# Routing 29 of 32 token tiles before the block boundary, with constant matmuls on a waiting TensorE

## The chip, the cores and the metric

The kernel runs on one core of a Trainium2 chip. The metric is the device time of one execution in microseconds, and lower is better. Three runs of the kernel before took 1498.8, 1500.05 and 1500.13 us; the median is 1500.05. The engines are TensorE (PE in the rows, with PEld for its weight loads), VectorE (DVE), ScalarE (ACT), GpSimd (POOL) and SyncE (SP), which here issues DMAs.

## The reference

The input x has 8 x 512 rows of 1024 numbers. Two stages are added to it one after the other:

```python
x = x + tanh(g_xattn) * long_conv(ctx, ctx, layernorm(x), ssm_kernel, D)   # head size 8
x = x + tanh(g_ffn) * moe(layernorm(x), G, gate_w, up_w, down_w, lora_A, lora_B)
```

The long convolution stands where attention would: the products of keys and values within a head are convolved with a kernel of 1024 steps and contracted with the queries. In the mixture of experts each of the 4096 rows (tokens) gets scores by a softmax over 8 experts; its two best experts (the first of equals) each compute down(silu(gate x) * (up x)) with 128 hidden units and a low-rank term of rank 16, weighted by the score:

```python
scores = softmax(x @ G); value, indices = top_k(scores, 2)
w = sum_k value_k * one_hot(indices_k)
out = einsum('bsef,bse,ehf->bsh', silu(gate) * up, w, down_w) + lora term
```

## The kernel before

The kernel is written directly for the engines: each has its own list of instructions, and semaphores order them. There are two blocks. At the end of a block all engines meet (line L199 in the rows), so that no engine starts the second block before all have issued what they have in the first.

**First block, `attend`.** It runs over 32 tiles (NT) of 128 rows: two plain passes, a loop, and two plain ones for tiles 30 and 31. Per tile TensorE computes the convolution as fp32r products of 288 columns (`conv`, `shared`), VectorE multiplies with the queries and sums (`multiply`, `total`, `residual`), ScalarE and GpSimd split numbers in high and low parts. One and two tiles later follow the second norm (`root2`, `invert2`, `normalize2`), its transposes (`transpose_n2`), the high and low parts (`high_n2`, `low_n2`), and the product with G (`project`, `take_small`, `turn`, `take_lr`), which leaves the tile's 8 logits per token in `logits`. After tile 31's convolution this tail runs once more with nothing beside it. SyncE stores the new x and the normed rows n2 of tile 31 and waits until they have landed.

**Second block, `route_tokens`, then `experts_on_slots`.** The routing computes, for all 32 tiles at once and for 256 elements per partition, the softmax and the two one-hot choices (VectorE, about 20 operations that each wait for the one before), and counts on TensorE (CNT) how many tokens go to each expert ahead of each token. From the counts it makes each choice's slot tile and row in it. It then builds `is_slot` and `is_row` on VectorE (L947, L952), multiplies is_slot by the token's number on GpSimd (`slot_number`, L1018), and 64 matmuls of 72 columns (IDX, L1054) turn them into the list of tokens per slot. From IDX come `token` (L966), which GpSimd's indirect DMAs need to gather rows (L826), and the tables of experts and waits (L971 to L978), which end with `tables_done`. Only then do the slots start: 71 slots of 128 rows, each transposed (L1228), multiplied with its expert's weights (L1241 to L1260) and scattered (L1112). The gathered row holds the token's 8 weights as well, so that the gathers wait until they have been stored (`weight_out`, L987).

SyncE in the second block first copies rows to a spare place (L981), loads two experts' weights (L813), waits for each, stores the weights of the routing (L987), and then issues the packs: 16 DMAs of 64 KB (`pack`, L799) that bring the low-rank matrices, split in high and low parts by the first block, together in DRAM, from where `load_b` takes them (L804).

Of the kernel before, what the change touches and what calls it, by code (L numbers as in the profile page):

```python
# [21 lines left out]
F32 = mybir.dt.float32  # L22
# [43 lines left out]
BACK = SLOTS // NB  # L66

# [6 lines left out]
class Constants:  # L74


    def __init__(self, nc, ctx, g_xattn, g_ffn, ident, order, utri, ones, iota, grid, number):
# [7 lines left out]
        self.first = [(self.ident, ident), (self.g_xattn, g_xattn)]  # L85
        self.later = [(self.g_ffn, g_ffn), (self.order, order), (self.utri, utri), (self.ones, ones), (self.iota, iota),
# [3 lines left out]
def attend(nc, logits, constants, x_d, c_d, k_d, dskip_d, ag_d, w_d, khi_d, klo_d, kshi_d, kslo_d, out_d, normed_d, whi_d, wlo_d):  # L90
# [3 lines left out]
    with ctx:  # L94
# [8 lines left out]
        kvhi = [sb(f"kvhi{h}", [P, NC, YC], F32R) for h in range(HT)]  # L103
        kvlo = [sb(f"kvlo{h}", [P, NC, YC], F32R) for h in range(HT)]
# [41 lines left out]
        shared_y = view(OP[:], [[HALF, 2], [1, YC]])  # L146

# [43 lines left out]
        q_done = sem("q_done")  # L191

# [6 lines left out]
        with nc.Block() as block:  # L199

            @block.sync
            def _(eng):
# [64 lines left out]
                body(NT - 1, 1, last=True)  # L267
                eng.wait_ge(res_done, NT)
# [6 lines left out]
                eng.wait_ge(w_out, 32 * NT)  # L275
                eng.wait_ge(later_in, 16 * len(constants.later))

            @block.gpsimd
            def _(eng):
# [50 lines left out]

                head(0, 0, 0, 16)

# [12 lines left out]
                body(NT - 1, 1, NT // 2 - 1, last=True)  # L345

            @block.scalar
            def _(eng):
# [110 lines left out]
                eng.wait_ge(const_in, 48)  # L459
                nc.scalar.activation(gt[:], gate[:], ACT.Tanh).then_inc(gate_ready, 1)  # L460
                nc.scalar.copy(ag_parts[:, :, 0, :], ag[:]).then_inc(ag_split, 1)
# [5 lines left out]
                def body(i, p, k, first=False, last=False):  # L467
# [11 lines left out]
                    take_common(2 * i + 1, 1)  # L479
                    if not last:  # L480
                        head(2 * i + 2, 1 - p, 0)
# [12 lines left out]
                body(NT - 1, 1, NT // 2 - 1, last=True)  # L494
                take_small(NT - 2)
                root2(NT - 1, 1)
                normalize2(NT - 1, 1)
                high_n2(NT - 1)
                take_small(NT - 1)

            @block.vector
            def _(eng):
# [86 lines left out]
                def body(i, p, k, first=False, last=False):  # L589
# [19 lines left out]
                    total(i, p, 1, 0)  # L609
                    if not first:  # L610
                        low_n2(i - 1)
# [11 lines left out]
                body(NT - 2, 0, NT // 2 - 1)  # L623
# [6 lines left out]
                take_lr(NT - 1)  # L630

            @block.tensor
            def _(eng):
# [90 lines left out]
                eng.wait_ge(const_in, 48)  # L724
# [31 lines left out]
                body(NT - 1, 1, last=True)  # L756
                transpose_o(NT - 1, 1)
                project(NT - 2)
                turn(NT - 2)
                transpose_n2(NT - 1, 1)  # L760
                project(NT - 1)
                turn(NT - 1)


class Chosen:


    def __init__(self, nc, ctx):
        sb = lambda n, s, dt=F32: ctx.enter_context(nc.sbuf_tensor(n, s, dt))
        U32 = mybir.dt.uint32  # L770
        self.token, self.dest = sb("token", [P, SG], U32), sb("dest", [P, SG], U32)
        self.spare_out, self.tables_done = ctx.enter_context(nc.semaphore("spare_out")), ctx.enter_context(nc.semaphore("tables_done"))
        self.need = sb("need", [P, NB, SG], mybir.dt.int32)
        self.opened = sb("opened", [1, NB, E])
        self.scattered = [ctx.enter_context(nc.semaphore(f"scattered{b}")) for b in range(NB)]
        self.own = sb("own", [P, SG, E])
        self.table = sb("table", [P, 2, SG], mybir.dt.int32)
        self.ends = sb("ends", [P, E], mybir.dt.int32)


class Weights:


    def __init__(self, nc, ctx):
        sb = lambda n, s, dt=F32: ctx.enter_context(nc.sbuf_tensor(n, s, dt))
        self.hi = sb("wt_hi", [P, 2, WC], F32R)
        self.lo = sb("wt_lo", [P, 2, WC], F32R)
        self.lb = ctx.enter_context(nc.sbuf_tensor("lora_b", [P, 2, L], F32R))
        self.landed = ctx.enter_context(nc.semaphore("weights_landed"))
        self.lb_zero = ctx.enter_context(nc.semaphore("lb_zero"))  # L790
        self.lb_landed = ctx.enter_context(nc.semaphore("lb_landed"))
        self.packed = ctx.enter_context(nc.semaphore("packed"))

    def pack(self, eng, w_d, b_d, e):

        part = bass.AP(tensor=w_d.tensor, offset=w_d.offset + NT // E * e * P * WT + WQ,
                       ap=[[WT, P], [P * WT, NT // E], [1, BQ]])
        to = bass.AP(tensor=b_d.tensor, offset=b_d.offset + e * R * L, ap=[[NT // E * BQ, P], [BQ, NT // E], [1, BQ]])
        eng.dma_start(to, part).then_inc(self.packed, 16)  # L799

    def load_b(self, eng, bhi_d, blo_d, e):

        for n, d in enumerate((bhi_d, bhi_d, blo_d)):
            eng.dma_start(self.lb[n * ST:n * ST + R, e % 2, :].bitcast(F32), d[e]).then_inc(self.lb_landed, 16)  # L804

    def load(self, eng, whi_d, wlo_d, e, singly=False):
# [597 lines left out]
```

## Time and profile before

| | us |
|---|---|
| median of three runs | 1500.05 |
| the profiled execution | 1499.49 |
| its span, first to last instruction | 1497.7 |
| TensorE busy | 1398.2 (93%) |
| VectorE busy | 1152.2 (77%) |
| ScalarE busy | 774.7 (52%) |
| GpSimd busy | 1117.3 (75%) |
| mean granted TensorE clock | 0.970 of 2.4 GHz |

The profile shows one execution. Its 40 slices of 37.4 us each give the busy share of each engine in tenths:

```profile
PE   3999999999999999999999999933899999999994
DVE  3999999999999999999999999958354454445452
POOL 6998999899899989998999899515355555555552
PEclk9999999999999999999999999955999999999997
```

A 9 is 90% or more. TensorE is full everywhere but at the start, at the end and in two slices between the attention and the slots, where the granted clock (PEclk, in tenths of full) is also low. The time is thus the sum of two stages that TensorE bounds and of the stretch between them.

### The profile page before, as it was taken

The page shows a single profiled execution, that of the slowest core. Times are in us where ns is not written, and L with a number is a line of the kernel's source. Part 1 is how long each engine was busy: PE and PEld are TensorE (multiplying, and loading weights), DVE is VectorE, ACT ScalarE, POOL GpSimd, SP SyncE. Part 2 cuts the span into 40 slices and gives each one's busy share as a digit, 9 for nine tenths or more (in the row PEclk, how much of TensorE's full clock was granted, in tenths as well). Part 3 has the DMA queues.
Part 4 walks back from the last instruction along what each step waited for, and adds up shares of the span by engine and source line. Part 5 has one row for each costly group of instructions (what it writes and reads, how often), then busy time and mean ns, then how long its engine had stood idle before and what let it go on. Part 6 is the DMA issues. An engine that isn't in the chain of part 4 may idle for free. (4 is left out here: it accounts for less than half of the span.)

```text
span 1497.7 us, 33735 instructions
## 1 busy us (share of the span) xinstructions
PE 1398.2 (93%) x10290; PEld 1347.3 (90%) x10291; DVE 1152.2 (77%) x1922; ACT 774.7 (52%) x1359; POOL 1117.3 (75%) x985
## 2 busy tenths in 40 slices
PE   3999999999999999999999999933899999999994
PEld 3999999999999999999999999923899999999994
DVE  3999999999999999999999999958354454445452
ACT  5656665666566656665666566410333443343341
POOL 6998999899899989998999899515355555555552
PEclk9999999999999999999999999955999999999997
DMA  6766675777676767676767676436589999999984
GB/s 202 206 217 224 213 229 207 231 207 234 204 228 210 235 201 226 211 228 210 227 210 233 203 226 212 161 130 169 120 199 251 267 232 238 250 271 217 234 179 72
DMA packets 114342, 315.44 MB, mean 211 GB/s; under 512 B 25152, under 2 KB 25664, under 8 KB 114304
## 3 DMA queue, kind: packets, MB, share of 16 engines
q1 hardware_dynamic: 93728, 239.96, 50.9%
q0 software_dynamic: 20576, 75.04, 22.4%
q8 instruction: 16, 0.26, 0.1%
q14 instruction: 22, 0.18, 0.0%
HBM read 215.66 MB, written 100.86 MB: 211 GB/s over the span
## 5 line engine op out<-in xcount | busy, mean ns | idle before, releaser
L536 DVE TENSOR_REDUCE oT<-z 128x128 f32<-128x1280 f32 x256 | 380.5, 1486 | 8.9
L637 PE MATMUL Y<-kvhi,t_hi 128*128 128x288 f32 x1280 | 382.5, 299 | 0.0
L638 PE MATMUL Y<-kvlo,t_hi 128*128 128x288 f32 x1280 | 377.7, 295 | 0.0
L639 PE MATMUL Y<-kvhi,t_lo 128*128 128x288 f32 x1280 | 377.1, 295 | 0.0
L309 POOL TENSOR_TENSOR kvlo<-kv,kvhi 128x1152 fp32r<-128x1152 f32 x128 | 340.7, 2686 | 0.0
L292 POOL TENSOR_TENSOR kv<-cT 128x768 f32<-128x768 f32 x128 | 239.1, 1868 | 9.1 <-DMA cT<-in_c 9.1
L637 PEld LDWEIGHTS Y<-kvhi,t_hi 128*128 128x128 f32 x1280 | 240.5, 188 | 0.6
L638 PEld LDWEIGHTS Y<-kvlo,t_hi 128*128 128x128 f32 x1280 | 240.8, 188 | 0.0
L639 PEld LDWEIGHTS Y<-kvhi,t_lo 128*128 128x128 f32 x1280 | 240.8, 188 | 0.0
L519 DVE TENSOR_TENSOR z<-Y,qT 128x512 f32<-128x512 f32 x256 | 176.8, 691 | 28.2 <-PE Y L639 16.2
L1241 PE MATMUL GU<-wt_hi,xu_hi 128*128 x568 | 170.5, 300 | 0.0
L1243 PE MATMUL GU<-wt_lo,xu_hi 128*128 x568 | 164.4, 290 | 0.0
L1242 PE MATMUL GU<-wt_hi,xu_lo 128*128 x568 | 163.5, 288 | 0.0
L637 PE MATMUL Y<-kvhi,u_hi 128*128 128x288 f32 x512 | 155.0, 303 | 0.0
L1109 POOL TENSOR_TENSOR clear<-own 1x1 f32<-1x1 f32 x284 | 44.2, 183 | 144.2 <-issue 115.1
L639 PE MATMUL Y<-kvhi,u_lo 128*128 128x288 f32 x512 | 151.3, 295 | 0.0
L638 PE MATMUL Y<-kvlo,u_hi 128*128 128x288 f32 x512 | 151.1, 295 | 0.0
L303 POOL TENSOR_TENSOR diff<-kv 128x576 f32<-128x576 f32 x64 | 92.1, 1439 | 65.8 <-ACT kv L353 62.9
L364 ACT CAST kvhi<-kv 128x1152 fp32r<-128x1152 f32 x128 | 140.8, 1149 | 0.4 <-POOL kv L295 0.4
L522 DVE TENSOR_TENSOR z<-Y,qT 128x384 f32<-128x384 f32 x256 | 140.4, 549 | 0.0
L1112 POOL DMA_INDIRECT out<-made,dest x71 | 113.0, 1591 | 27.0 <-issue 19.7
L515 DVE TENSOR_TENSOR Y<-Y,common 128x576 f32<-128x576 f32 x128 | 97.9, 765 | 36.1 <-PE Y L639 36.1
(174 smaller groups left out, 3266.4 us busy)
## 6 DMA issues: line engine op xcount, KB each, us to landing
cT<-in_c SPq DMA_DIRECT2D x32, 768.0 KB, 8.0
t_hi<-khi SPq DMA_DIRECT2D x64, 384.0 KB, 3.6
t_lo<-klo SPq DMA_DIRECT2D x64, 384.0 KB, 5.0
u_hi<-kshi SPq DMA_DIRECT2D x64, 320.0 KB, 5.8
u_lo<-kslo SPq DMA_DIRECT2D x64, 320.0 KB, 6.8
x_nat<-in_x SPq DMA_DIRECT2D x32, 512.0 KB, 4.1
out<-x_new SPq DMA_DIRECT2D x32, 512.0 KB, 4.8
normed<-n SPq DMA_DIRECT2D x32, 512.0 KB, 7.4
```

The costliest lines, as they stand in the source:

```text
L292: nc.gpsimd.tensor_tensor(view(o, [[YC, NC // 2], [IB, ND - 1], [1, IB]], IB), view(cc, [[WR, NC // 2], [0, ND - 1], [1, IB]]), view(cc, [ ...
L309: nc.gpsimd.tensor_tensor(kvlo[h][:, c0:c0 + NC // 2, :], kv[:, c0:c0 + NC // 2, :], kvhi[h][:, c0:c0 + NC // 2, :].bitcast(F32), ALU.subt ...
L364: nc.scalar.copy(kvhi[h][:, c0:c0 + NC // 2, :], kv[:, c0:c0 + NC // 2, :]).then_inc(kvhi_done, 1)
L519: nc.vector.tensor_tensor(view(zz, [[ZC, 2], [2 * SK, ND], [2, IB]]), view(y, [[HALF, 2], [IB, ND], [1, IB]]), view(q, [[WR, 2], [0, ND], ...
L522: nc.vector.tensor_tensor(view(zz, [[ZC, 2], [2 * IB, ND - 1], [2, IB]], 1), view(y, [[HALF, 2], [IB, ND - 1], [1, IB]], IB), view(q, [[WR ...
L536: nc.vector.tensor_reduce(oT[p][:, 2 * r:2 * r + 2, h * IB:(h + 1) * IB], view(z[s][:], [[ZC, 2], [2, IB], [2 * IB, ZS], [1, 2]]), AX.XY, ...
L637: nc.tensor.matmul(out, w_hi[:, w], m_hi[:, c, :], start=start, stop=False)
L638: nc.tensor.matmul(out, w_hi[:, w], m_lo[:, c, :], start=False, stop=False)
L639: return nc.tensor.matmul(out, w_lo[:, w], m_hi[:, c, :], start=False, stop=stop)
L1241: nc.tensor.matmul(out, xt_hi[p][:, c, :], wh, start=c == 0, stop=False)
L1242: nc.tensor.matmul(out, xt_lo[p][:, c, :], wh, start=False, stop=False)
L1243: mm = nc.tensor.matmul(out, xt_hi[p][:, c, :], wl, start=False, stop=c == NC - 1)
```

## The change

The change does the following.

- **29 tiles routed in the first block.** TE is 29, TL is 3. Tiles 0 to 28 (early) get their softmax, choices, counts and places within `attend`: `start_early` in VectorE's tile 30, Exp in ScalarE's tile 31, the rest between the steps of tile 31's tail, and their counts in TensorE's tail into a free half of Y[0]. GpSimd multiplies the early weights (`product`) and makes the early row matrices of two of four pieces (`number_rows`, 29 operations of 128 elements) before the blocks meet.
- **3 tiles late.** The second block handles tiles 29 to 31 in operations of 24 elements, and one matmul brings in the early sums. The prefix sum over the experts takes two operations instead of eight.
- **The number moves.** The row matrix now holds the token's number (is_equal, then mult, in one operation), in the buffers of kvhi and kvlo; `slot_number` on GpSimd falls away. One of the four pieces is made on ScalarE as Square and Relu (32 operations), the others on GpSimd.
- **SyncE.** In the first block it now waits for the early weights, stores them, and only then stores x and n2 of tile 31; after their landing it issues all 16 packs. In the second block it waits for the packs, then loads, with the late weights' store in between.
- **Constant products.** `keep_busy` issues matmuls of 256 columns whose output nothing reads: 40 before transpose_o of tile 31, 30 before transpose_n2, 3 before the last turn; in the second block 25 before the late counts, 40 before IDX, 55 after it.
- **Small things.** g_ffn is loaded with the first constants and its tanh taken at the start; Sqrt and Exp on dummy values load ScalarE's tables ahead of their use; `Weights` and `Chosen` move up in the file.

The core of the diff:

```diff
+TE = NT - 3
+TL = NT - TE
+def keep_busy(nc, out, weights, moving, count):
+    for _ in range(count):
+        nc.tensor.matmul(out, weights, moving, start=True, stop=True)
+FIRST_ROWS = ((1, 0), (0, 1))
+def split_places(nc, eng, routed, part, done):
+    V = nc.vector
+    V.tensor_copy(routed.block_i[:, :, part], routed.place[:, :, part]).then_inc(routed.split, 1)
...
+    V.tensor_copy(routed.row[:, :, part], routed.row_i[:, :, part]).then_inc(routed.cast, 1)
...
+def number_rows(engine, routed, constants, c, half, within):
+    tiles = [t for t in range(half * NT // 2, (half + 1) * NT // 2) if within.start <= t < within.stop]
+    for t in tiles:
+        ins = engine.tensor_scalar(routed.numbered(c, t), constants.iota[:], routed.row[:, c, t:t + 1],
+                                   constants.number[:, t:t + 1], ALU.is_equal, ALU.mult)
+    ins.then_inc(routed.rows_done[c][half], 1)
...
             @block.sync
                 body(NT - 1, 1, last=True)
+                eng.wait_ge(weighted, 1)
+                eng.dma_start(weight_d[:, early], routed.weight[:, early]).then_inc(routed.weight_out, 16)
                 eng.wait_ge(res_done, NT)
                 eng.dma_start(out_d[NT - 1], x_new[1][:]).then_inc(x_out[1], 16)
...
                 eng.wait_ge(w_out, 32 * NT)
+                for e in range(E):
+                    weights.pack(eng, whi_d, bhi_d, e)
+                    weights.pack(eng, wlo_d, blo_d, e)
...
+                def route_early():
+                    eng.wait_ge(routed.gate_done, 1)
+                    nc.gpsimd.memset(weights.lb[:].bitcast(F32), 0.0).then_inc(weights.lb_zero, 1)
+                    nc.gpsimd.memset(routed.weight[:, late], 0.0).then_inc(routed.cleared, 1)
+                    nc.gpsimd.memset(routed.chosen[:, late].bitcast(F32), 0.0).then_inc(chosen_zero, 1)
+                    eng.wait_ge(sums_done, 1)
+                    nc.gpsimd.tensor_tensor(product[:], routed.scores[:, early], routed.chosen[:, early].bitcast(F32),
+                                            ALU.mult).then_inc(product_done, 1)
+                    eng.wait_ge(routed.cast, 1)
+                    for c, half in FIRST_ROWS:
+                        number_rows(nc.gpsimd, routed, constants, c, half, early)
...
             @block.scalar
+                nc.scalar.copy(routed.utri, constants.utri[:]).then_inc(sums_ready, 1)
+                nc.scalar.copy(routed.ones, constants.ones[:]).then_inc(sums_ready, 1)
+                nc.scalar.activation(dcol[:], epsc[0:NH, :], ACT.Sqrt)
                 take_small(NT - 2)
                 root2(NT - 1, 1)
                 normalize2(NT - 1, 1)
                 high_n2(NT - 1)
+                nc.scalar.activation(dcol[:], epsc[0:NH, :], ACT.Exp)
+                eng.wait_ge(weight_zero, 1)
+                eng.wait_ge(product_done, 1)
+                nc.scalar.mul(routed.weight[:, early, 0:E], product, routed.gate[:, 0:1]).then_inc(weighted, 1)
                 take_small(NT - 1)
...
             @block.vector
                 total(NT - 1, 1, 1, 3)
+                scale_early()
                 residual(NT - 1, 1)
+                choose_early(0)
+                invert2(NT - 1)
+                choose_early(1)
+                count_early()
                 take_lr(NT - 2)
-                invert2(NT - 1)
                 low_n2(NT - 1)
+                place_early()
                 take_lr(NT - 1)
...
             @block.tensor
+                eng.wait_ge(z_done, 8 * NT - 1)
+                idle(40)
                 transpose_o(NT - 1, 1)
                 project(NT - 2)
                 turn(NT - 2)
+                idle(30)
                 transpose_n2(NT - 1, 1)
...
                 project(NT - 1)
+                idle(3)
                 turn(NT - 1)
...
     def route_sync(eng):
+        eng.wait_ge(weights.packed, 32 * E)
+        weights.load(eng, whi_d, wlo_d, 0)
+        weights.load_b(eng, bhi_d, blo_d, 0)
+        eng.wait_ge(weighted, 1)
+        eng.dma_start(weight_d[:, late], routed.weight[:, late]).then_inc(routed.weight_out, 16)
+        eng.wait_ge(weights.landed, LANDED)
+        eng.wait_ge(weights.lb_landed, 48)
+        weights.load(eng, whi_d, wlo_d, 1)
         eng.dma_start(spare_d, normed_d[0:P, 0:L]).then_inc(spare_out, 16)
...
     def route_gpsimd(eng):
+        number_rows(nc.gpsimd, routed, constants, 1, 1, early)
+        eng.wait_ge(routed.cast, 2)
+        number_rows(nc.gpsimd, routed, constants, 0, 1, late)
+        number_rows(nc.gpsimd, routed, constants, 1, 1, late)
         for b in range(NB):
             eng.dma_start(keep.opened[0:1, b, :], normed_d[0:1, 0:E]).then_inc(keep.scattered[b], 16)
...
-        eng.wait_ge(weight_out, 16)
+        eng.wait_ge(routed.weight_out, 32)
...
     def route_tensor(eng):
+        nc.tensor.matmul(CNT[:, 0:(TL + 1) * E], routed.ones, routed.sums[:].rearrange("p (o e) -> p o e", o=1)
+                         .to_broadcast([P, TL + 1, E]), start=True, stop=False)
+        idle(25)
         eng.wait_ge(rt, at["chosen"])
...
+        idle(40)
+        for c, half in PIECES:
+            eng.wait_ge(routed.rows_done[c][half], waits[c, half])
+            eng.wait_ge(slots_done[c][half], 1)
+            for t in range(half * NT // 2, min((half + 1) * NT // 2, TE)):
+                nc.tensor.matmul(IDX[:, 0:SG], routed.numbered(c, t), is_slot[:, c, t, :], start=first, stop=False)
...
         mm.then_inc(idx_done, 1)
+        idle(55)
```

## Rows read from the trace of the kernel before

**Rows 1.** Busy time by stages: window, length, engines (instructions), granted clock, DMA share, GB/s.

```profile
976.00:996.90 20.90, 8.91 (x36) 5.88 (x36) 8.27 (x14) 4.91 (x9) 0.00 (x0) 0.61 0.13 51
996.90:1017.50 20.60, 2.69 (x12) 2.64 (x12) 16.43 (x49) 2.19 (x5) 4.51 (x6) 0.50 0.80 277
1017.50:1040.20 22.70, 14.52 (x64) 13.95 (x64) 21.78 (x12) 0.00 (x0) 16.42 (x4) 0.50 0.49 116
1040.20:1048.10 7.90, 0.00 (x0) 0.00 (x0) 4.05 (x12) 0.00 (x0) 3.95 (x5) 0.50 0.79 211
1048.10:1060.70 12.60, 7.88 (x44) 7.32 (x45) 2.82 (x5) 3.78 (x5) 0.94 (x1) 0.70 0.28 96
1060.70:1464.00 403.30, 403.30 (x2854) 378.06 (x2853) 198.05 (x475) 158.80 (x339) 213.98 (x405) 1.00 0.92 226
```

**Rows 2.** The chain that ended last, at the token and the slots' first transpose.

```profile
1040.20 0.24 DVE token L966
...
1048.16 1.96 PE XU L1228 x8
```

**Rows 3.** Busy time in short windows, columns as in group 1, for the clock.

```profile
980.00:981.00 1.00, 0.00 (x0) 0.00 (x0) 1.00 (x1) 0.00 (x0) 0.00 (x0) 0.79 0.00 0
1021.00:1029.60 8.60, 7.25 (x32) 6.97 (x32) 8.60 (x3) 0.00 (x0) 6.10 (x3) 0.50 0.49 64
1054.10:1055.60 1.50, 1.50 (x8) 1.50 (x7) 0.00 (x0) 1.01 (x1) 0.00 (x0) 0.50 0.04 11
1055.60:1058.00 2.40, 2.40 (x20) 2.28 (x18) 1.31 (x3) 0.00 (x0) 0.26 (x1) 0.99 0.00 0
```

**Rows 4.** SyncE at the meeting of the engines, and n2's last store (L271).

```profile
L199 SPq DRAIN  x1: 7/7/7, 993.6 to 993.6; - x1
...
L199 SPq EVENT_SEMAPHORE  x1: 17/17/17, 996.8 to 996.8; - x1
...
DMA to landing us min/median/max: 4.2/4.2/4.2
```

**Rows 5.** Timeline of the attention's end: start, length, engine, line, operation, [idle before].

```profile
981.34 1.97 PE L695 MATMUL OP<-const_ident,oT 128*128 128x128 f32 x8 [5.36 <-DVE oT L536]
...
983.35 1.28 DVE L550 SCALAR_TENSOR_TENSOR x_new<-OP,gt,x_nat 128x1024 f32<-128x1024 f32 x1 [2.06 <-PE OP L695]
...
996.92 1.28 ACT L1002 ACT_TABLE_LOAD   x1 [1.26 <-PEq L199]
```

**Rows 6.** SyncE's issues: two in the timeline, and line L799 (ns min/median/max).

```profile
989.02 0.33 SPq L271 DMA_DIRECT2D normed<-n  x1
...
1021.73 0.41 SPq L987 DMA_DIRECT2D normed<-wt  x1
...
L799 SPq DMA_DIRECT2D bhi<-whi x8: 548/635/2797, 1022.2 to 1042.2; - x8
```

**Rows 7.** Timeline of VectorE's small operations in the routing: 256 and 8 elements.

```profile
1000.49 0.42 DVE L909 TENSOR_TENSOR tb<-sc,top 128x256 f32<-128x256 f32 x1
...
1009.59 0.17 DVE L930 TENSOR_SCALAR nti<-nti 128x8 int32<-128x8 int32 x1
```

**Rows 8.** GpSimd's lines L295 and L1018, and VectorE's two is_slot in the timeline.

```profile
L295 POOL TENSOR_TENSOR kv<-cT x128: 443/466/523, 11.3 to 947.3; 128x128 f32<-128x128 f32 x128
...
L1018 POOL TENSOR_TENSOR slot_number<-is_slot,const_number x4: 4086/4122/4157, 1017.6 to 1032.3; 128x1152 fp32r<-128x1152 f32 x4
...
1014.92 2.56 DVE L947 TENSOR_TENSOR is_slot<-slot_f,const_grid 128x2304 f32<-128x2304 f32 x1
...
1023.72 4.47 DVE L947 TENSOR_TENSOR is_slot<-slot_f,const_grid 128x2304 f32<-128x2304 f32 x1
```

**Rows 9.** Issue to landing: the gathers (L826), the opened DMAs (L1012), packs (L799).

```profile
DMA to landing us min/median/max: 4.3/7.1/10.1
...
DMA to landing us min/median/max: 5.8/5.9/6.1
...
DMA to landing us min/median/max: 2.4/2.9/7.0
```

More of the change, by code:

```diff
@@ L146, in attend @@
         shared_y = view(OP[:], [[HALF, 2], [1, YC]])
+        early, late = routed.early, routed.late
+        free = qT[0][:].rearrange("p h c w -> p (h c w)")
+        left, mark, product = [free[:, n * TE * E:(n + 1) * TE * E].rearrange("p (t e) -> p t e", e=E) for n in range(3)]
+        ranked = free[:, 3 * TE * E:5 * TE * E].rearrange("p (c t e) -> p c t e", c=2, e=E)
+        best = routed.place[:, 0, early]
+        CNT = Y[0][:, 0, 0:NT * E]
         later_in = sem("later_in")
@@ L761, in _ @@
+                for s in range(1, NT // GT):
+                    mm = nc.tensor.matmul(grouped[:, s:NT // GT], routed.ones,
+                                          groups[:, 0:NT // GT - s, :].rearrange("p g (o e) -> p g o e", o=1)
+                                          .to_broadcast([P, NT // GT - s, GT, E]), start=False, stop=s == NT // GT - 1)
+                mm.then_inc(early_counted, 1)
                 project(NT - 1)
+                idle(3)
                 turn(NT - 1)
[L765 to L778, printed above, removed]
@@ L940, in route_vector @@
[L940 to L955 removed]
+        link(V.tensor_tensor(sums[:], routed.before[:], nt[:].rearrange("p (o e) -> p o e", o=1).to_broadcast([P, E, E]), ALU.mult))
@@ new lines, in route_vector @@
+        link(V.tensor_reduce(slot[:].rearrange("p c t -> p (c t)"), opening[:], AX.X, ALU.add))
+        eng.wait_ge(routed.blocks, 2)
+        link(V.tensor_tensor(slot[:], slot[:], routed.block[:], ALU.add))
+        for c, half in PIECES:
+            part = slice(half * NT // 2, (half + 1) * NT // 2)
+            V.tensor_tensor(is_slot[:, c, part], slot[:, c, part].rearrange("p (t o) -> p t o", o=1).to_broadcast([P, NT // 2, SG]),
+                            grid[:].rearrange("p (o s) -> p o s", o=1).to_broadcast([P, NT // 2, SG]),
+                            ALU.is_equal).then_inc(slots_done[c][half], 1)
@@ L1042, in route_tensor, with idle @@
[L1042 to L1055 removed]
+        def idle(count):
+            keep_busy(nc, UNUSED[:, 0:2 * P], routed.ones, routed.both[:], count)
@@ new lines, in route_tensor @@
+        waits = {(1, 0): 1, (0, 1): 1, (1, 1): 1, (0, 0): 1}
+        first = True
+        idle(40)
+        for c, half in PIECES:
+            eng.wait_ge(routed.rows_done[c][half], waits[c, half])
+            eng.wait_ge(slots_done[c][half], 1)
+            for t in range(half * NT // 2, min((half + 1) * NT // 2, TE)):
+                nc.tensor.matmul(IDX[:, 0:SG], routed.numbered(c, t), is_slot[:, c, t, :], start=first, stop=False)
+                first = False
+        for c in range(2):
+            eng.wait_ge(routed.rows_done[c][1], 2)
+            for t in range(TE, NT):
+                mm = nc.tensor.matmul(IDX[:, 0:SG], routed.numbered(c, t), is_slot[:, c, t, :], start=False,
+                                      stop=c == 1 and t == NT - 1)
```

412 lines of the change are left out of this document (242 added, 170 removed).

## The prediction

> **What bounds the kernel now.** I read the table by stages first [rows 1]. TensorE works without a gap in the attention, up to 976, and in the experts' slots, from 1060.7 to 1464. Between them lie 84.8 us in which it is mostly idle: the last tile's tail (20.9 us), the routing up to the slot tables (20.6 + 22.7 us), the first gathers (7.9 us) and the cold start of the slots (12.6 us). In the attention nothing but spare time of VectorE is touched and the slots keep their work, so I worked through the junction alone. The chain of waits there runs through VectorE's chain of small operations, GpSimd's two pairs of slot_number products (16.4 us busy), the 64 IDX matmuls and the token, which is made at 1040.2; the slots' first transpose follows at 1048.16 [rows 2]. The clock is at 1.2 GHz from 980.6 to 1055.6 [rows 3].
>
> A point that the chain does not show: between the attention's block and the routing's block all engines meet. SyncE had drained at 993.6, and its event came at 996.8, with the last of the others [rows 4]. Whatever the change puts into the first block delays everything behind that meeting, on whichever engine it stands. I call the meeting's time B: 996.9 now.
>
> **The attention's end after the change.** Start_early adds two VectorE operations of 0.4 us to tile 30, and Exp with its table load (1.7 us) stands in ScalarE's spare time before high_n2(30); VectorE waits for TensorE there anyway. I cost them at nothing; without that cover it would be 0.9 us.
> TensorE's 40 constant products start at 977.0, when tile 31's z of step 2 is done. A 272-column product takes 0.12 us at 2.4 GHz (20 in 2.4 us, [rows 3]), so 40 take 4.8 us and end at 981.8, 0.5 us after transpose_o starts now [rows 5]. The clock fell only within 980 to 981, 4 us and more after TensorE's last product at 976 [rows 3], so it is kept, and the eight transposes take 1.0 us for 1.97: the residual starts at 982.9 for 983.35 [rows 5]. Then on VectorE: residual to 984.2, the first choice (6 x 0.41) to 986.7, invert2, the second choice (5 x 0.41) and the counts to 990.4, low_n2 to 991.9. Normalize2 ends at 988.6, the transposes at 989.6, high_n2 at 990.7. ScalarE then loads Exp's table (1.28, [rows 5]) and multiplies: the early weights are ready at 992.7. Place_early and the split (464 elements twice, five small ones) put the row numbers at 994.0, and VectorE is done at 994.8. Every compute engine but GpSimd would thus be ready 2 us sooner than now.
>
> SyncE would not. Its order is: wait for the early weights, store them, then store x_new and n2 of tile 31 (both were ready at 984.2 and 988.6), wait for the landings, then issue 16 packs, which before stood behind the meeting. Step by step: 992.7; the store of 29 x 64-byte pieces per partition holds the queue like the one of 32 did, 0.41 us and 2.2 of the next issue's 2.80; x_new's issue takes 0.33, so n2's store is issued at 995.6 [rows 6]; it lands in 4.2 when alone [rows 4] and, I estimate, 0.7 later behind x_new's 512 KB, at 1000.5; 16 packs at 0.635 are 10.2, with small gaps 11.0 us [rows 6]. **B is 1011.5**, 14.6 us later than now. Bounds: 1009.5 (no gaps, and x_new's store costs n2's nothing) and 1013 (two stores of 512 KB queued behind small pieces).
> GpSimd has 29 tensor_scalar of 128 elements in the same stretch, from 994.1. No row shows that operation. From below: a fraction of L295's two-input product of 128 elements, 0.2 us; near it: 0.47 us less overlap, 0.44; from above: no row bars 1 us. I take 0.44, the row nearest in shape: 12.8 us, ready at 1006.9 and hidden behind SyncE. The cover ends at 0.59 us each. The Trainium skill (GPSIMD Engine Reference, 4.1 Engine selection) calls GpSimd's one-input work roughly line-rate; by that it would end near 1001. No run so far shows it.
>
> **The routing after B.** Operations of 24 elements take 0.17 us, with the link 0.195, where 256 elements took 0.42 [rows 7]. Sixteen of them and Exp make the late tiles' choice in 3.8 us. TensorE was idle for 17 us before B, so its 25 constant products start at 1.2 GHz: 0.213 us each, 5.3 us, perhaps the last few faster. Counts are thus ready at B+6.4, bound by the constant products and not by the choice. The port matters here too: the second is_slot took 4.47 us where the first took 2.56, and it ended 2.4 us after the GpSimd product beside it [rows 8]; nine two-input operations beside GpSimd's 13 number_rows may each wait some 0.25 us, so the choice ends at up to B+6.1, still at the same time as the constant products.
> The Trainium skill (SBUF, Who interferes with whom) says that a VectorE instruction with two SBUF inputs and a GpSimd one that reads SBUF block each other in whole; the trace agrees with 4.47 for 2.56. Without such a lock the sum would be the same, for TensorE ends at that time.
> Then: tile counts and begins 1.2 us, late places 0.4, split 0.9, opening 1.6, with 0.4 for the port: B+10.9. Four is_slot of 1152 elements, half of 2.56 each [rows 8]: B+12.2, 13.5, 14.8, 16.0. Slot_number is gone, since the row matrices now hold the number: that takes 16.4 us of GpSimd off the chain and is the change's main gain. IDX keeps 64 products. At 1.2 GHz 32 took 7.25 us [rows 3]; at 2.4 GHz 64 take that, if the 40 constant products have brought and kept the whole clock: from B+12.2 to B+19.4. VectorE's table chain (3.1 us without GpSimd) ends at B+19.1. The token comes at **B+19.5**, for B+43.3 now: 23.8 us saved, 14.6 given back at B, net 9.2.
>
> The 32 row operations on ScalarE (0.2 us each) end near B+12 and are hidden. GpSimd after B: 13 x 0.41 beside the choice, from B+8.9 six more (2.5), the four opened DMAs (2.8), landing 5.9 [rows 9]: B+20.1, which is just before the first gather would issue (token + 1.17, B+20.7). At 0.6 us each it would hold the gather for 0.6. SyncE waits for the last pack's landing, 2.9 [rows 9], and then loads two experts' weights, so that the second's come beside the first gathers.
>
> **The slots' start.** From token to first transpose 7.96 us go by, set by the need tables [rows 2]. The gather must land in 6.8; in the slots, beside weights, gathers took 4.3 to 10.1, median 7.1 [rows 9]. I add 0.5. The 55 constant products (6.6 us) keep the clock until 1.5 us before that transpose. If it stays whole to the first product, the two sets of transposes lose 0.9 us each and the first seven products 0.1 each, 2.6 us together; if it falls between them, 0.9. I take 1.5. **Sum:** 9.2 - 0.5 + 1.5 = 10.2 off 1499.5, the profiled execution: 1489.3. That execution is 0.5 us under the median of the runs, so I forecast **1489.8**.
>
> **The rivals.** (1) The clock does not hold in IDX. For it: two runs of 16 such products, 7.25 us of work in 8.6, left it at 1.2 GHz [rows 3]. Against it: nothing in the trace shows what they do to a clock that is whole. If it falls halfway, IDX takes 3.6 us more and the 55 products some 2 more, partly behind the token's 8 us: 1494. If it is half from the start, IDX takes 14.5 and the 55 products (11.7 us) outlast the 8: 10.9 us more, 1500.7. Chance 0.22, mostly for the first.
> (2) Slower: GpSimd's price. At p us each the block ends at 994.4 + 29p, once p is over 0.59, and after B come 19p, the opened DMAs (8.7) and the gather (6.8) before the first transpose. At p = 0.8 that is 1017.6 + 30.7 = 1048.3, no gain but the clock; from about 0.85 on the kernel is slower; at 1.0 it is 1023.4 + 34.5, 9.7 us late, 1508. For it: each operation takes two values per partition and two steps, which no row has. Against it: L295 with two inputs takes 0.47 [rows 8]. Chance 0.10.
> (3) The packs do not hold the meeting, since the queue takes them faster or the stores land sooner: B at 1007, where GpSimd ends. 4.5 us less, 1485. For it: a plain store issues in 0.33; against it: the packs' own least is 0.55, which would give only 1009 [rows 6]. Chance 0.08.
> (4) The gathers or the opened DMAs hold the first transpose, beside the weights: landing at 10.1 instead of 7.1, 3 us, 1493. Chance 0.12.
> The forecast itself has 0.48.
>
> **How the numbers follow.** The likeliest case spans 1486 to 1493. The range takes in (3) and (4) and the half-falling clock: **1484 to 1497**. A difference under 0.2% (3 us) cannot be told from none here. Faster by more needs a time under 1497.05: 0.48 + 0.08 + 0.12 + 0.17 of rival 1, and 0.01: 0.86, less 0.03 for what is overlooked, **0.83**. Within 0.2%: **0.06**. Slower: **0.11**, nearly all rival 2, with rival 1 at its end.
>
> **What the new profile would show.** The first operation after the meeting at 1011 to 1012, with SyncE's event last and its packs before it; number_rows at 0.4 us in a row; the granted clock whole from 977 to about 997, half at B, whole again from B+5 or so to the end of IDX; slot_number gone; the token some 19.5 us after B; slots from the 2nd on at 5.94 us as now (403.3 us for 68, [rows 1]). I would be wrong if GpSimd is the last at the meeting, if IDX runs at 0.22 us a product, or if the attention up to 976 has moved by more than 0.5 us.

## The result, and the profile after

The changed kernel takes 1510.18 us (median of 7 runs, 1507.79 to 1512.32), beside 1500.05 us for the kernel before (7 runs). The ratio is 1.0063, with a 95% interval of 1.0053 to 1.0072: slower by 10 us, where 10 us faster was forecast. The time lies outside the range.

| | before | after |
|---|---|---|
| profiled execution, us | 1499.5 | 1510.2 |
| its span, us | 1497.7 | 1508.4 |
| TensorE busy, us | 1398.2 | 1420.9 |
| GpSimd busy, us | 1117.3 | 1148.7 |
| mean granted clock | 0.970 | 0.978 |

The 40 slices of the page after, 37.7 us each:

```profile
PE   4999999999999999999999999947899999999994
DVE  3999999999999999999999999935344445455452
POOL 6998998999899989998999999457355555555552
PEclk9999999999999999999999999977899999999998
```

The slices between attention and slots have more TensorE work and a higher clock than before (7, 7, 8 for 5, 5), and the stretch is no shorter. The table by stages says where the time went. Columns are as in [rows 1]; the windows are the last tile's tail up to the meeting, the routing up to the token, up to the first slot's transpose, the cold start, and the slots:

```profile
977.70:1021.30 43.60, 17.75 (x121) 16.05 (x120) 16.87 (x39) 6.88 (x12) 23.24 (x30) 0.71 0.27 54
1021.30:1044.10 22.80, 21.56 (x135) 21.41 (x136) 16.61 (x49) 9.79 (x34) 22.65 (x23) 0.72 0.78 264
1044.10:1056.80 12.70, 8.16 (x56) 7.95 (x55) 4.05 (x12) 0.00 (x0) 4.10 (x6) 0.77 0.68 225
1056.80:1069.40 12.60, 7.88 (x44) 7.33 (x45) 2.82 (x5) 3.78 (x5) 0.94 (x1) 0.70 0.25 83
1069.40:1472.70 403.30, 403.30 (x2846) 375.49 (x2845) 197.94 (x474) 158.56 (x337) 213.99 (x401) 1.00 0.93 226
```

The meeting moved from 996.9 to 1021.3, 24.4 us later, 1.7 of them already in the attention. The routing from meeting to token shrank from 43.3 to 22.8 us, 20.5 less. From token to first transpose it grew from 7.9 to 12.7, 4.8 more. The cold start is as cold and as long as before (0.70, 12.6 us). Together 8.7 us: the first transpose is at 1056.86 for 1048.16. The other 2.0 us of the span lie behind it and say nothing: that rest took 448.1 to 453.8 us in the profiled executions of all the kernels below, 449.5 in the kernel before and 451.5 in this one.

Who held the meeting stands in the view of its line, L349 now (count, ns min/median/max, start):

```profile
L349 ACTq DRAIN  x1: 391/391/391, 998.4 to 998.4; - x1
L349 DVEq DRAIN  x1: 17/17/17, 1000.1 to 1000.1; - x1
L349 POOLq DRAIN  x1: 9377/9377/9377, 1011.8 to 1011.8; - x1
L349 SPq DRAIN  x1: 204/204/204, 1015.1 to 1015.1; - x1
L349 SPq EVENT_SEMAPHORE  x1: 17/17/17, 1021.3 to 1021.3; - x1
```

[rows 4] is the same view before. GpSimd is last: its sequencer waits 9.4 us for its own queue, until 1021.2. ScalarE and VectorE came at 998.4 and 1000.1, SyncE at 1015.1. The cause is in the view of line L98, the row operations, and in GpSimd's timeline (start, length, operation, [idle before]):

```profile
L98 POOL TENSOR_SCALAR kvlo<-const_iota,row_f,const_number x32: 783/792/4300, 1011.0 to 1041.1; 128x128 fp32r<-128x128 f32 x32
L98 POOL TENSOR_SCALAR kvhi<-const_iota,row_f,const_number x16: 783/784/813, 998.5 to 1010.2; 128x128 fp32r<-128x128 f32 x16
```
```profile
998.49 12.47 POOL L98 TENSOR_SCALAR kvhi<-const_iota,row_f,const_number 128x128 fp32r<-128x128 f32 x16 [5.56 <-DVE row_f L89]
1010.96 10.10 POOL L98 TENSOR_SCALAR kvlo<-const_iota,row_f,const_number 128x128 fp32r<-128x128 f32 x13
1021.44 20.46 POOL L98 TENSOR_SCALAR kvlo<-const_iota,row_f,const_number 128x128 fp32r<-128x128 f32 x19 [0.38 <-POOLq L349]
1041.85 2.37 POOL L1197 DMA_DIRECT2D opened<-normed  x4
```

One operation takes 0.78 us, not 0.44, and the first starts at 998.5, not 994.1. The chain of waits from the meeting to the first transpose does not pass through the token at all. It is GpSimd's queue nearly to its end: 19 row operations, the issues of the opened DMAs, their landing, the first two gathers. Behind the second gather GpSimd signals VectorE (`issued`), which only then makes the need tables that the first slot waits for, 3.3 us:

```profile
1021.44 20.46 POOL kvlo L98 x19
1041.90 0.75 POOL opened L1197
...
1043.71 5.32 DMA opened<-normed
...
1050.04 1.04 POOL slot_rows L188
...
1055.47 0.32 DVE need L1155
...
1056.86 1.96 PE XU L1410 x8
```

The token was there at 1044.1, so that a free GpSimd would have issued that gather at 1045.3 instead of 1050.0.

### The profile page after: what moved, and what is told of

Its sections match the earlier page's. It is cut to its first block and busy times, and to the rows that moved or that the text cites. A ratio compares the mean times of both kernels' runs of the same rounds, so it can differ in the third digit from the quotient of the medians.

```text
span 1508.4 us, 34238 instructions
## 1 busy us (share of the span) xinstructions
PE 1420.9 (94%) x10487; PEld 1368.8 (91%) x10488; DVE 1142.8 (76%) x1938; ACT 788.2 (52%) x1398; POOL 1148.7 (76%) x1032
## 5 line engine op out<-in xcount | busy, mean ns | idle before, releaser
L464 POOL TENSOR_TENSOR kvlo<-kv,kvhi 128x1152 fp32r<-128x1152 f32 x128 | 344.2, 2714 | 0.0
```

What stands on the lines that cost most here:

```text
L464: nc.gpsimd.tensor_tensor(kvlo[h][:, c0:c0 + NC // 2, :], kv[:, c0:c0 + NC // 2, :], kvhi[h][:, c0:c0 + NC // 2, :].bitcast(F32), ALU.subt ...
```

## The experiments

My theory after this reading: GpSimd's price (rival 2) makes the change a loss, and behind it stand, hidden from the time, SyncE's packs and two small delays in the first block. The rival theories were that the constant products cost something, and that GpSimd's price matters only beside those others. All kernels were timed beside the kernel before. "First transpose" is that of the first slot. No kernel leaves out part of the computation; e4_no_constants and e8_together_no_constants leave out the constant products, whose output nothing reads.

**The rows on VectorE.** The 29 operations before the meeting move to the end of VectorE's first block; the 19 after it stay on GpSimd.

```diff
-                    for c, half in FIRST_ROWS:
-                        number_rows(nc.gpsimd, routed, constants, c, half, early)
...
+                for c, half in FIRST_ROWS:
+                    number_rows(nc.vector, routed, constants, c, half, early)
```

> The changed kernel with the 29 early row operations before the meeting issued by VectorE behind its other work instead of by GpSimd. Theory (GpSimd is last at the meeting because of 29 x 0.78 us): the meeting falls back from 1021.4 to where SyncE's 16 packs end, 1015.2, and all after it moves by as much: 6 us faster than the changed kernel, 1504. One such operation on VectorE should take under 0.3 us. Rival (VectorE pays as much for them as GpSimd, 0.7 us or more): no difference or slower.

Measured: 1503.89 us (8 runs), ratio 1.0026 (1.0016 to 1.0037), 6.3 us less than the changed kernel; first transpose at 1050.86, 6.0 sooner. VectorE's view of the line, and the meeting:

```profile
L98 DVE TENSOR_SCALAR kvhi<-const_iota,row_f,const_number x16: 335/338/345, 998.0 to 1001.9; 128x128 fp32r<-128x128 f32 x16
```
```profile
L349 SPq DRAIN  x1: 205/205/205, 1014.3 to 1014.3; - x1
```

The same operation takes 0.335 us on VectorE, and 16 of them 4.19 us, 0.26 apiece. Now SyncE is last, as the prediction had it for 1011.5: its packs end at 1014.1 and it drains at 1014.3, where GpSimd had drained by 992.8. The meeting is 6.2 us sooner, and so is the time. But the kernel is still slower than before, by two things: the packs, and GpSimd's 19 other rows, behind which the gather still waits (1044.06).

**The packs sooner.** The kernel of the run above, with SyncE issuing the packs while it waits for tile 31's x_new, whose waits it has anyway, and the early weights' store last.

```diff
+                eng.wait_ge(w_out, 32 * NT)
+                for e in range(E):
+                    weights.pack(eng, whi_d, bhi_d, e)
+                    weights.pack(eng, wlo_d, blo_d, e)
                 eng.wait_ge(res_done, NT)
...
+                eng.wait_ge(weighted, 1)
+                eng.dma_start(weight_d[:, early], routed.weight[:, early]).then_inc(routed.weight_out, 16)
```

> As e3 (early rows before the meeting on VectorE), and SyncE in another order: the 16 packs are issued while it waits for tile 31's x_new, then the stores of x_new and n2, and the early weights' store last. Theory (once GpSimd is out of the way the meeting is set by SyncE's weights store, landing wait and packs, as the prediction had it at 1015): the meeting falls from 1015.1 to where VectorE's rows end, 1005.6, 9 us faster than e3, 1495. Rival (what e3 gained was the whole of it; the second block's weights or gathers would hold the slots at the same time): no faster than e3, 1504.

Measured: 1496.73 us (5 runs), ratio 0.9968 (0.9955 to 0.9982), 7.2 us less than without this edit and, for the first time, under the kernel before. The size is near the expected. The profiled execution is the longest of the five (1502.64); its attention ended 6.2 us later than in the run above (40 constant products from 984.74 for 978.59), for a cause that I don't know. Counted from there, the meeting comes 8.9 us sooner than in the run above (27.5 us for 36.4), as expected, with VectorE's rows last. What is left is GpSimd's, in its timeline:

```profile
1012.45 19.98 POOL L98 TENSOR_SCALAR kvlo<-const_iota,row_f,const_number 128x128 fp32r<-128x128 f32 x19 [13.56 <-POOLq L349]
...
1042.27 1.04 POOL L188 DMA_INDIRECT slot_rows<-normed,token  x1 [7.52 <-issue]
```

**The opened DMAs first.** In the changed kernel, the four opened DMAs go ahead of the 19 rows.

```diff
     def route_gpsimd(eng):
+        for b in range(NB):
+            eng.dma_start(keep.opened[0:1, b, :], normed_d[0:1, 0:E]).then_inc(keep.scattered[b], 16)
         number_rows(nc.gpsimd, routed, constants, 1, 1, early)
```

> The changed kernel with one move: GpSimd issues the four small opened DMAs at the start of the second block, ahead of its 19 row operations, and not behind them. Theory (GpSimd's row operations at 0.78 us and what is queued behind them hold the first gather): the opened DMAs no longer land last, but their issue puts the rows 2.4 us later, so the late IDX products end near 1045.2, the token follows at 1045.5 and the first gather at 1046.7 instead of 1050.0: 3 to 4 us faster than the changed kernel, some 1507. Rival (the weights' landing or the gathers' own landing would hold the slots anyway): no difference to the changed kernel, 1510.

Measured: 1506.49 us (4 runs), ratio 1.0047 (1.0031 to 1.0064), 3.7 us less than the changed kernel, but only 1.1 of it by the first transpose. TensorE's timeline:

```profile
1045.98 1.48 PE L1236 MATMUL IDX<-is_slot,kvlo 128*128 128x72 f32 x6
1047.26 8.65 PE L74 MATMUL UNUSED<-utri_ones 128*128 128x256 f32 x55
1055.75 1.03 PE L1410 MATMUL XU<-const_ident,slot_rows 128*128 128x128 f32 x8
```

The wait moved: the rows start 3.2 us later, IDX ends as much later, and the token comes at 1047.5. The 55 constant products now end just as the rows arrive and bring a whole clock to the slots, 1.03 us for the eight transposes, not 1.94; that is the 1.5 us or so that the prediction wanted from them. The rest of the 3.7 is within what the profiled executions differ by.

**The last logits' wait sooner.** VectorE takes tile 30's logits between the first choice and invert2, not behind the counts.

```diff
                 choose_early(0)
+                take_lr(NT - 2)
                 invert2(NT - 1)
                 choose_early(1)
                 count_early()
-                take_lr(NT - 2)
```

> The changed kernel with one move: in VectorE's tail of the first block take_lr(30) stands behind the first choice and not behind the second choice and the counts. Theory (transpose_n2 of tile 31 waited for take_lr(30), 2.3 us idle in which the clock fell to 1.2 GHz): it starts near 990.4 instead of 992.4 at 2.4 GHz, the places and the first GpSimd row come 3 us sooner, and since GpSimd is the last at the meeting, the whole kernel is about 3 us faster than the changed one, 1507. Rival (SyncE's packs, which ended at 1014.9, or something else sets the meeting): no difference.

Measured: 1507.39 us (4 runs), ratio 1.0052 (1.0035 to 1.0069), 2.8 us less. The timeline of TensorE, first of the changed kernel, then of this one:

```profile
992.42 1.66 PE L945 MATMUL XP<-const_ident,n 128*128 128x128 f32 x8 [2.31 <-DVE logits L747]
```
```profile
990.16 1.09 PE L945 MATMUL XP<-const_ident,n 128*128 128x128 f32 x8 [0.38 <-ACT n L579]
```

transpose_n2 of tile 31 writes a bank that take_lr of tile 30 must have read. The change put take_lr behind the second choice and the counts, and TensorE waited 2.3 us for it, with n2 ready at 990.4. Just behind that wait the clock fell (granted 1.00 in 991 to 992, 0.87 in 992 to 993, 0.50 after) and the transposes took 1.66 for 1.09. The fall does not come with the wait each time: in e3_rows_on_vector, with the same 2.31 us, they took 1.06. Here GpSimd's first row starts at 995.67 for 998.49, and the first transpose of the slots at 1053.58.

**The subtraction on GpSimd.** start_early's subtraction of the largest logit goes from VectorE's tile 30 to GpSimd behind its work for tile 31.

```diff
-                    V.tensor_tensor(sc, logits[:, early], tokens(best), ALU.subtract).then_inc(less_done, 1)
...
+                    nc.gpsimd.tensor_tensor(routed.scores[:, early], logits[:, early],
+                                            best.rearrange("p (t o) -> p t o", o=1).to_broadcast([P, TE, E]),
+                                            ALU.subtract).then_inc(less_done, 1)
```

> The changed kernel with the early scores' subtraction of the maximum moved from VectorE in tile 30 (where it took 2.21 us for 232 elements beside GpSimd's work, against 0.40 for the same form elsewhere) to GpSimd behind its last tile. Theory (the attention ended 1.7 us later because this operation waited for GpSimd's use of the shared port, longer than VectorE's slack): the last convolution product starts at 975.8 again and not at 977.4. Rival (another cause, as the longer instruction stream): it stays at 977.4. The maximum itself stays on VectorE (0.39 us).

Measured: 1507.27 us (one run, 0.5 below the lowest of the changed kernel, so that the time alone shows little), first transpose at 1053.86, 3.0 sooner. VectorE's timeline in the changed kernel, and where TensorE's attention ends in each (the 40 constant products start when it has):

```profile
940.00 2.21 DVE L786 TENSOR_TENSOR scores<-logits,place 128x232 f32<-128x232 f32 x1
...
978.78 5.05 PE L74 MATMUL Y<-t_hi 128*128 128x256 f32 x40 [1.05 <-DVE z L705]
```
```profile
976.04 5.06 PE L74 MATMUL Y<-t_hi 128*128 128x256 f32 x40 [1.05 <-DVE z L709]
```

A two-input operation of 232 elements, estimated at 0.4 us, took 2.2 beside a busy GpSimd: it ended at 942.2, GpSimd's product beside it (L464) at 941.95. VectorE had less spare time than I thought; TensorE then waited 0.5 and 1.2 us for it, waits that neither the kernel before nor this run has. Without it the attention ends 2.7 us sooner, and this is no accident of one execution: the 40 constant products start at 978.4 to 979.3 in the changed kernel, e1, e2 and e3, and at 975.9 to 976.7 in the four kernels here that have them and the subtraction on GpSimd. On GpSimd the same operation takes 0.59.

**No constant products.** All loops of keep_busy empty, once on the changed kernel (e4), once on the next one (e8).

```diff
-    for _ in range(count):
+    for _ in range(0):
```

> The changed kernel without any of the products of constants that keep TensorE busy (all counts zero), all else alike. Theory (TensorE's clock is not what holds this junction now; GpSimd's rows and the opened DMAs are): the transposes and projections of the first block's tail run at 1.2 GHz, the places come up to 1 us later, IDX runs at 1.2 GHz but still waits for the late rows: within 2 us of the changed kernel, 1510 to 1512. Rival 1 (the constants hold real work up): 3 us or more faster. Rival 2 (the kept clock is worth its 8 or more us): 1518 or more.

Measured: 1511.09 us (4 runs), ratio 1.0082 (1.0065 to 1.0099), 0.9 above the changed kernel, not to be told from none. IDX takes 13.9 us (64 products at 1.2 GHz) for 10.6, and it doesn't matter, since GpSimd's queue holds the first transpose (1057.35). The constant products cost nothing and gave nothing here.

**All together.** The logits' wait, the subtraction and the packs as above. Rows before the meeting: VectorE makes the two pieces (1, 0) and (1, 1), GpSimd piece (0, 1), 29 and 13 of them side by side. After it GpSimd has the opened DMAs and six late rows only.

```diff
-                    for c, half in FIRST_ROWS:
-                        number_rows(nc.gpsimd, routed, constants, c, half, early)
+                    number_rows(nc.gpsimd, routed, constants, 0, 1, early)
...
+                for c, half in ((1, 0), (1, 1)):
+                    number_rows(nc.vector, routed, constants, c, half, early)
...
     def route_gpsimd(eng):
-        number_rows(nc.gpsimd, routed, constants, 1, 1, early)
+        for b in range(NB):
+            eng.dma_start(keep.opened[0:1, b, :], normed_d[0:1, 0:E]).then_inc(keep.scattered[b], 16)
```

> The changed kernel with all that the runs so far point to: take_lr(30) sooner, the subtraction on GpSimd, SyncE's packs sooner, the row operations before the meeting shared (29 on VectorE, pieces (1,0) and (1,1); 13 on GpSimd, piece (0,1)), and GpSimd in the second block issuing the opened DMAs first and only the 6 late rows. Theory: the meeting at about 1004.6, the token 20 to 22.5 us behind it (the latter if the clock falls within IDX as it did at 1037.1 in the changed kernel), the first slot transpose at 1032 to 1035: 1485 to 1488, faster than both kernels. Rival (the weights of two experts, the gathers or the clock set the slots' start): 1495 or more.

Measured: 1488.22 us (5 runs), ratio 0.9922 (0.9909 to 0.9936): 12 us faster than the kernel before, 22 faster than the changed one. The chain of waits from the meeting (1004.9) on has no GpSimd in it; its long pieces:

```profile
1005.37 4.42 PE UNUSED L74 x25
...
1014.45 1.37 DVE is_slot L1134
...
1015.96 10.25 PE IDX L1235 x58
1026.21 1.28 PE IDX L1240 x6
1027.49 8.77 PE UNUSED L74 x55
1036.25 0.89 PE XU L1414 x8
```

The meeting itself is still GpSimd's: its 13 rows end at 1004.6, VectorE's 29 at 1002.4.

The short windows of this kernel show the clock in IDX (columns as in [rows 1]):

```profile
1016.00:1018.00 2.00, 2.00 (x19) 2.00 (x19) 2.00 (x2) 0.00 (x0) 2.00 (x1) 1.00 0.19 46
1018.00:1020.00 2.00, 2.00 (x14) 2.00 (x14) 2.00 (x3) 0.00 (x0) 2.00 (x2) 0.62 0.26 45
1020.00:1022.00 2.00, 2.00 (x12) 2.00 (x11) 1.86 (x5) 0.00 (x0) 2.00 (x3) 0.50 1.01 356
```

The clock is whole when IDX starts and falls to 1.2 GHz some 2.5 us into it, though TensorE is busy without a gap. So 64 products take 11.5 us, where 7.25 were forecast.

> As e7 without any product of constants. Theory (with GpSimd's rows off the chain IDX is on it, so that its clock matters now): the counts come 1 us sooner, the 64 IDX products take 14.5 us instead of 7.3 to 10.5, so 3 to 6 us slower than e7, 1490 to 1493. Rival (the constants are worth nothing here either): as e7.

Measured, the same without constant products: 1492.00 us (5 runs), ratio 0.9945 (0.9931 to 0.9958). With GpSimd out of the way the constant products are worth 3.8 us: IDX takes 13.8 us for 11.5, and the first slot's transposes 1.94 for 1.03.

**The price alone.** The kernel of e7_together, but with the rows where the change has them, 29 on GpSimd before the meeting and 19 after it, behind the opened DMAs.

```diff
-                    number_rows(nc.gpsimd, routed, constants, 0, 1, early)
+                    for c, half in FIRST_ROWS:
+                        number_rows(nc.gpsimd, routed, constants, c, half, early)
-                for c, half in ((1, 0), (1, 1)):
-                    number_rows(nc.vector, routed, constants, c, half, early)
...
+        number_rows(nc.gpsimd, routed, constants, 1, 1, early)
```

> All of e7_together, but the row operations stand on GpSimd as in the changed kernel: 29 before the meeting, 19 early ones after it (behind the four opened DMAs), no row operation of an early tile on VectorE. It prices GpSimd's row operations with the other costs gone. Theory, 0.79 to 0.82 us each: the 29 start at 994 and end at 1017.5, which is the meeting (e7: 1004.9); the token follows 26 us after it, as in e1_opened_first, at 1043.5, and the first slot at 1051.5, for 1036.1 in e7. In all 1503.5 us: the whole of e7's gain over the kernel before is gone, and more. Rival, the price matters only beside the packs and the late attention's end: the kernel then stays under 1495 us.

Measured: 1502.14 us (10 runs), ratio 1.0017 (1.0007 to 1.0027). The chain of waits:

```profile
1019.03 6.38 POOL kvlo L98 x9
...
1026.57 7.83 POOL kvlo L98 x4
...
1034.44 6.40 PE IDX L1234 x29
```

The meeting is at 1015.9 for 1004.9, and IDX now waits for the 13 early rows among the 19; the first transpose comes at 1050.18, 13.9 us later than in e7_together, and the whole takes 13.9 us more. So where these 48 operations stand (29 of them change their engine) alone decides between a gain of 0.8% and a loss of 0.2%, with the packs and the small delays out of the way.

**Fewer constant products.** e7_together with fewer of them before the counts and after IDX.

```diff
-        idle(25)
+        idle(16)
...
-        idle(55)
+        idle(46)
```

> All of e7_together, with 16 constant products for 25 before the late counts and 46 for 55 after IDX. Theory, constant products are only worth having as long as they end before the work that they stand ahead of: in e7 the 25 ended 1.2 us after the late tiles' choice was ready (1010.2 for 1009.0), and the 55 ended at 1036.25, 0.75 us after the first slot's rows had come. With fewer, the counts start 1.2 us sooner and the first slot 0.7 us sooner on top: first slot transpose near 1034.3, 1486.5 us in all for 1488.2. Rival, the 9 fewer leave the clock at 1.2 GHz in IDX or at the slots' start: IDX takes 3 us more or the first slot 2 us more, and the kernel takes 1489 to 1491.

Measured: 1487.65 us (4 runs, 1483.61 to 1488.78), ratio 0.9918 (0.9902 to 0.9935). It can't be told from e7_together by its time. The trace shows what was meant: the counts follow the choice at once (at 1008.2), the clock at the slots' start is still whole, and the end of the chain is now the gather's landing:

```profile
1026.60 6.42 DMA slot_rows<-normed,token
...
1033.45 1.08 PE XU L1414 x8
```

The first transpose is 2.8 us sooner than in e7_together, 0.8 of it from an attention that ended sooner. Whether the 2 us are a gain stays open.

## Why the prediction was wrong, point by point

**What bounds it, and the meeting.** Right in kind: the attention and the slots kept their periods, and everything turned on the junction and on what the first block holds back. The two sums that were at stake were both placed there, and the wrong one was taken as hidden.

**The price of GpSimd's row operation** is the step that failed, and with it the step that took GpSimd as hidden behind SyncE at the meeting. I took 0.44 us from L295, the row nearest in shape [rows 8], with "the cover ends at 0.59". It is 0.78 (29 in 22.6 us). An estimate that the whole sign hangs on was taken from a different operation, a two-input product; this one has two values per partition and two steps, the very point that I had named for the rival and given 0.10. The Trainium skill (GPSIMD Engine Reference, 4.1 Engine selection), by which I had added that the block would end near 1001, speaks of one-input work as roughly line-rate; here the operation takes 2.3 times VectorE's 0.335, and the measurement decides.

**Rival 2** is what happened, and it was itself priced too low: for 0.8 us it gave a first transpose at 1048.3. At the measured 0.78 it gives 1017.0 + 30.3 = 1047.3, and 1056.86 was measured. Of the missing 9.5 us, 4.3 lie at the meeting, since the rows started 4.1 later than its 994.4, and 5.7 in the 19 rows, 20.5 us for 14.8. One of them took 4.3 us beside VectorE's four is_slot (3.5 too many), the next 2.1, and two others 1.3 and 1.0, each beside an operation of VectorE. The opened DMAs and the gather behind them took 15.0 for 15.5. So the price of 0.78 alone takes the forecast gain away, since 1047.3 is where the kernel before stands (1048.16); the loss of 10 us needed the late start and the waits beside VectorE too.

**The attention's end.** Two additions costed at nothing were not. The subtraction made the attention 1.7 us later; I had written "VectorE waits for TensorE there anyway", with 0.9 as the other end, and such a wait was known from [rows 8], 4.47 us for 2.56. Here it was 2.21 for 0.40, to the end of a GpSimd instruction of 2.7 us (line L464, 2714 ns). The Trainium skill (SBUF, Who interferes with whom) states that lock; I weighed it for the routing and not here. And take_lr(30), listed in the diff as moved behind the counts, has a waiting engine behind it: TensorE's transpose_n2, 2.3 us, and in the changed kernel a fallen clock behind that. The early weights came at 997.0 for 992.7.

**SyncE and the packs.** Right: a pitch of 0.68 for 0.69, and the last pack done at 1014.9 for 1011.5, where 4.3 are the late weights and -0.9 the rest. Hidden in the changed kernel, and the bound as soon as GpSimd's rows are gone (e3_rows_on_vector). The forecast's meeting was a real second limit, not the first.

**The routing after the meeting.** The counts came at B+6.2 for 6.4, VectorE's table chain ended at B+19.1 for 19.1. IDX took 10.6 us for 7.25: rival 1, in its half-falling form, at 0.17 a fair chance. Token at B+22.8 for 19.5.

**The slots' start.** The whole clock for the first transposes (1.5 us) did not come in the changed kernel, since TensorE idled 4.6 us before them. It came where the constant products ended just ahead of the rows (e1_opened_first, e7_together).

**The sum again**, against the forecast of 1489.3 for the profiled execution: meeting 9.8, token 3.3, token to first transpose 4.3, clock 1.5, the rest of the slots 2.0: 20.9, which gives 1510.2. The token's 3.3 and the 4.3 behind it are one term, GpSimd's queue: IDX was 3.3 us too long, but e4_no_constants made it 3.3 us longer still and the time moved by 0.9 us, within the noise. The two rivals of probability 0.10 and 0.17 came together, and only the one of 0.10, rival 2, set the time. The 2.0 are not explained. Three small slips in the prediction change nothing: its stages between attention and slots add to 84.7 us, not 84.8; GpSimd's rows behind the meeting are counted at 0.41 us each and not at the 0.44 before it; and 403.3 us for 68 slots is 5.93 each.

**The range and the chances.** 1484 to 1497 left out the case that a term with no row of its own may be nearly twice its estimate. I had put the price's upper bound at 1 us in the text, worked out 1508 from it, and then let the range end at 1497. The rule that would have helped is the prediction's own: between bounds of 0.2 and 1 us, with the sign turning at 0.8 to 0.85, rival 2 was worth a chance of about a quarter.

## What to carry to other kernels

Before work is moved to a queue that all engines meet behind, price it with a row of the very operation and form; where there is none, its upper bound belongs in the range, and the sum must hold at that bound. Ask of each engine what its last item before the meeting is: here GpSimd's rows covered SyncE's packs, and only when both had gone (rows to VectorE, packs into SyncE's waiting time) did the time fall below the kernel before, by 4 us; with the late rows and the two delays mended too, the gain was 12. The constant products that keep TensorE's clock were worth 3.8 us where the next real work followed them at once, and nothing that could be measured as long as another queue ended later.

## What the runs showed of the hardware

- GpSimd's tensor_scalar with two values per partition takes 0.78 us for 128 elements, its product of two tensors of 128 elements 0.47 [rows 8]; VectorE takes 0.335 for the former, and 0.26 apiece in a row.
- Beside each other both engines lose: VectorE's subtraction of 232 elements took 2.21 us beside GpSimd's product, where a two-input product of the same size took 0.40 beside an idle GpSimd (L792), and the subtraction 0.59 on GpSimd itself; one row operation of GpSimd took 4.3 us while VectorE ran four is_slot of 1.3 us back to back, and six took 9.9 us in e7_together. VectorE's row operations beside GpSimd's took 0.39 for 0.335 (medians).
- IDX's products of 72 columns did not keep a whole clock: it fell 3.6 us into them in the changed kernel and some 2.5 us in e7_together, and some 2 to 3.4 us into them in each of the seven other runs in which IDX began at a whole clock, TensorE busy without a gap up to the fall in all of them. DMA traffic is not what they share: its share was 0.8 at the fall in the changed kernel and 0.00 in e7_together (1018.5 to 1019.0). Why it falls stays open. In the kernel before they ran at 1.2 GHz from the start and did not raise it [rows 3]. The changed kernel's short windows:

```profile
1036.00:1037.00 1.00, 1.00 (x12) 1.00 (x11) 1.00 (x1) 0.00 (x0) 1.00 (x2) 1.00 0.13 13
1037.00:1038.00 1.00, 1.00 (x8) 1.00 (x7) 0.97 (x3) 0.00 (x0) 1.00 (x1) 0.55 0.83 221
```
